# Weighted sum over edges: the weights move from the one-hots to the rows, which are split in two 12-bit parts

## What is computed

```python
msgs = x[edge_src] * edge_val[:, None]
agg = jax.ops.segment_sum(msgs, edge_dst, num_segments=x.shape[0])
return agg @ weight
```

## Time and profile before

| | us |
|---|---|
| median of three executions | 4533.24 |
| lowest, highest | 4529.37, 4536.89 |
| the profiled execution | 4536.84 |
| its span, from the first instruction to the last | 4535.1 |
| the pass, from its first gather to the start of its last addition | 1371.5 to 2025.1 |

### The profile page before, as it was taken

The page is one execution under the profiler, slowest core; times in us unless marked ns, Lnnn a source line. Parts: engine busy times, 40 slices in busy tenths (PEclk is TensorE's granted clock), DMA queues, the critical chain, the costliest instruction groups (busy, mean ns, idle before and its releaser), DMA issues. The chain is left out here.

```text
span 4535.1 us, 63274 instructions
## 1 busy us (share of the span) xinstructions
PE 3412.7 (75%) x19013; PEld 2743.6 (60%) x19013; DVE 2035.7 (45%) x5778; ACT 1546.3 (34%) x4091; POOL 2322.5 (51%) x2297
## 2 busy tenths in 40 slices
PE   3777787624396777774675399997978999998796
PEld 3555555412164555553564399996536888887696
DVE  4666555650144444442322211115346777777523
ACT  3554555410042222221221122221125666665432
POOL 3454555447505666653665544441427788885153
PEclk7888888756697888886788699998869999999698
DMA  6755555200005677660454487774549999997466
GB/s 188 220 163 145 154 159 144 57 11 14 0 24 187 224 234 233 229 203 29 129 167 151 132 246 236 243 241 146 133 125 252 257 262 263 266 264 173 133 214 206
DMA packets 491983, 777.54 MB, mean 171 GB/s; under 512 B 154329, under 2 KB 296994, under 8 KB 491394
## 3 DMA queue, kind: packets, MB, share of 16 engines
q1 hardware_dynamic: 359986, 498.14, 34.8%
q0 software_dynamic: 122608, 266.94, 24.1%
q10 hardware_dynamic: 9056, 8.43, 0.6%
HBM read 599.88 MB, written 173.38 MB: 171 GB/s over the span
## 5 line engine op out<-in xcount | busy, mean ns | idle before, releaser
L874 POOL DMA_INDIRECT sum_rows<-t_row,src_i x416 | 393.9, 947 | 401.5 <-POOLq L2143 157.5
L874 POOL DMA_INDIRECT ag_rows<-t_att,src_i x416 | 401.8, 966 | 378.8 <-DVE ag_msg L985 260.9
L1745 POOL DMA_INDIRECT eg_early<-t_edge,src_i x312 | 487.4, 1562 | 172.0 <-issue 88.5
L286 POOL DMA_INDIRECT t_cells<-times_seen,cell x416 | 404.5, 972 | 265.6 <-issue 126.8
L1065 PE MATMUL ps<-featT,ag_msg 128*128 128x128 f32 x1664 | 364.7, 353 | 126.9 <-issue 116.0
L1793 PE MATMUL ps<-eg_w,eg_rT 128*128 128x256 f32 x1664 | 435.2, 384 | 0.0
L1065 PEld LDWEIGHTS ps<-featT,ag_msg 128*128 128x128 f32 x1664 | 274.7, 235 | 230.2 <-issue 192.5
L1472 PE MATMUL ps<-cv_cells,cv_high 128*128 128x384 f32 (+2 forms) x1200 | 322.7, 349 | 95.4 <-DMA cv_cells<-t_cells 95.4
L971 DVE TENSOR_TENSOR att_sums<-att_sums,ps 128x384 f32 x416 | 228.7, 550 | 323.0 <-remote 148.1
L1113 PE MATMUL ps<-sum_w1g,sum_eaT 64*128 64x256 f32 x1248 | 217.1, 475 | 193.8 <-ACT sum_kept L1157 127.2
L1176 DVE TENSOR_TENSOR featT<-featT,ps 128x256 f32 x416 | 175.3, 421 | 366.0 <-remote 181.1
(11 more groups left out here) (434 smaller groups left out, 6803.8 us busy)
## 6 DMA issues: line engine op xcount, KB each, us to landing
cv_cells<-t_cells SPq DMA_DIRECT2D x225, 384.0 KB
t_pre<-sum_kept SPq DMA_DIRECT2D x156, 512.0 KB
eg_early<-t_pre SPq DMA_DIRECT2D x156, 512.0 KB
t_cells<-zeros SPq DMA_DIRECT2D x21, 1664.0 KB
cv_cells<-t_cells SPq DMA_DIRECT2D x75, 448.0 KB
xn<-in_L_ffn_W SPq DMA_DIRECT2D x57, 512.0 KB
xn<-in_L_ffn_expert_w SPq DMA_DIRECT2D x110, 256.0 KB
ag_trow<-t_dst SPq DMA_DIRECT2D x104, 256.0 KB
```

Source lines behind the costliest of these rows:

```text
L286: nc.gpsimd.indirect_dma_start(out=t_cells, out_offset=bass.IndirectOffsetOnAxis(ap=cell[:, c:c + 1], axis=0), in_=times_seen[:, c:c + 1], ...
L874: nc.gpsimd.indirect_dma_start(out=rows[:, j, :], out_offset=None, in_=table, in_offset=bass.IndirectOffsetOnAxis(ap=src_i[:, n:n + 1], ax ...
L1745: nc.gpsimd.indirect_dma_start(out=early[:, q % ES, n % 2, :], out_offset=None, in_=t_edge, in_offset=bass.IndirectOffsetOnAxis(ap=src_i[: ...
```

## The change

The weights leave the one-hots, which become plain 0 and 1 and are of type float32r. Instead the rows are weighted. ScalarE multiplies a gathered row by its edge's weight and rounds the result to float32r, the upper part `high`. VectorE computes row times weight less `high` in one instruction and rounds it to float32r too, the lower part `low`. Both have rings of HR = 8 buffers. TensorE then makes four float32r matmuls for each chunk where it made two of f32: upper and lower part for each half of the features, added up in PSUM.

The order on the engines changes with it. ScalarE weights chunk n+2 (AHEAD = 2) behind the copy of chunk n's pair. VectorE makes the lower part of chunk n+2 ahead of the addition of chunk n, and the four one-hots of a later lot behind the addition of the lot's last chunk. GpSimd may refill a row buffer after the lower part is made (`low_kept`), not after the product.

```diff
+            HR = 8
-            hot = sb(tag + "_hot", [EC, GR, EC], F32, c)
+            hot = sb(tag + "_hot", [EC, GR, EC], F32R, c)
+            high = sb(tag + "_high", [EC, HR, D], F32R, c)
+            low = sb(tag + "_low", [EC, HR, D], F32R, c)
...
+            AHEAD = 2
...
-                    gathers(pool, table, rows, GR, g.agg_ready)
+                    gathers(pool, table, rows, GR, g.low_kept)
...
-                    for l in range(EARLY):
+                    def keep(l):
                         if l >= KEPT:
                             act.wait_ge(slot_stored[l % KEPT].sem, slot_stored[l % KEPT].at(16 * (l // KEPT)))
                         act.wait_ge(g.pre_ready.sem, g.pre_ready.at(2 * l + 2))
                         nc.scalar.copy(kept[:, l % KEPT], ps[:, AB:AB + 2, :]).then_inc(g.hid_done.sem, 1)
 
+                    def upper_bits(n):
+                        act.wait_ge(gath[n % GR].sem, gath[n % GR].at(16 * (n // GR) + 16))
+                        if n >= HR:
+                            act.wait_ge(g.agg_ready.sem, g.agg_ready.at(n - HR + 1))
+                        nc.scalar.activation(high[:, n % HR, :], rows[:, n % GR, :], ACT.Identity, scale=weight[:, n:n + 1]).then_inc(g.high_kept.sem, 1)
+
+                    for n in range(AHEAD):
+                        upper_bits(n)
+                    for n in range(NCH):
+                        if n % 2 == 0 and not is_late(n // 2):
+                            keep(early_number(n // 2))
+                        if n + AHEAD < NCH:
+                            upper_bits(n + AHEAD)
...
-                            nc.vector.tensor_scalar(hot[:, ER * h + j, :], iota[:], dloc[:, bass.ds(ER * m + j, 1)],
-                                                    weight[:, bass.ds(ER * m + j, 1)], ALU.is_equal, ALU.mult).then_inc(g.one_hot.sem, 1)
...
+                            nc.vector.tensor_scalar(hot[:, n % GR, :], iota[:], dloc[:, n:n + 1], None, ALU.is_equal).then_inc(g.one_hot.sem, 1)
+
+                    def lower_bits(n):
+                        dve.wait_ge(g.high_kept.sem, g.high_kept.at(n + 1))
+                        nc.vector.scalar_tensor_tensor(low[:, n % HR, :], rows[:, n % GR, :], weight[:, n:n + 1], high[:, n % HR, :].bitcast(F32),
+                                                       ALU.mult, ALU.subtract).then_inc(g.low_kept.sem, 1)
...
+                    for m in range(LOTS - 1):
+                        one_hots(m)
+                    for n in range(AHEAD):
+                        lower_bits(n)
+                    for n in range(NCH):
+                        if n % ER == 0:
+                            windows[:] = starts(dve, nc.vector, n // ER)
+                        if n + AHEAD < NCH:
+                            lower_bits(n + AHEAD)
+                        add(n)
+                        if n % ER == ER - 1 and n // ER + LOTS - 1 < NL:
+                            one_hots(n // ER + LOTS - 1)
...
-                        pe.wait_ge(gath[j].sem, gath[j].at(16 * (n // GR) + 16))
+                        pe.wait_ge(g.low_kept.sem, g.low_kept.at(n + 1))
...
-                            lhs = rows[:, j, k * 128:(k + 1) * 128]
-                            mm = nc.tensor.matmul(ps[:, n % BANKS, k * EC:(k + 1) * EC], lhs, hot[:, j, :], start=True, stop=True)
+                            for which, split in enumerate((high, low)):
+                                mm = nc.tensor.matmul(ps[:, n % BANKS, k * EC:(k + 1) * EC], split[:, n % HR, k * 128:(k + 1) * 128], hot[:, j, :],
+                                                      start=(which == 0), stop=(which == 1))
```

More of the change, by code:

```diff
@@ L1162, in _, with one_hots @@
                     dve.wait_ge(g.added.sem, g.added.at(1))
-                    def one_hots(m, i, h, first):
+                    windows = []
+                    def one_hots(m):
                         for j in range(ER):
-                            nc.vector.tensor_scalar(hot[:, ER * h + j, :], iota[:], dloc[:, bass.ds(ER * m + j, 1)],
-                                                    weight[:, bass.ds(ER * m + j, 1)], ALU.is_equal, ALU.mult).then_inc(g.one_hot.sem, 1)
-                    def add(m, i, h, first):
-                        for j, b in enumerate(starts(dve, nc.vector, m)):
```

12 lines of the change are left out of this document (6 added, 6 removed).

## The result

The changed kernel is **slower**: 4623.92 us in the median of three runs (4611.07 to 4623.97) against 4533.24, a ratio of 1.0191 (95% interval 1.0161 to 1.0220). I had forecast 4478 us and a range up to 4556. Its profiled execution is the run of 4623.92 us.

What follows compares the result with a forecast made beforehand. GpSimd's gather issue was taken as the floor, with late TensorE results holding the pass above it: 10.3 + 1.0 = 11.3 us per 8 chunks, 588 + 11 = 599 us against 654, so 4478 us; range 4415 to 4556.

Steps and rivals of the forecast that it cites:

- The price of the products: PE's weighted-sum matmuls: four single-pass products cost 0.27 us per chunk instead of 0.50, with 0.45 as upper end.
- The clock: PE in the edited pass: busy share falls from 70% to about 50%, granted clock 0.77 beside 0.85 before.
- rival 3: PE at 1.2 GHz for most of the pass; ScalarE's copy loop takes 12.5 us per 8 chunks: 4540 us; chance 0.12.
- rival 4: PE: float32r products of 128 columns cost 0.45 us per chunk, PE nearly as busy as now; shares 0.22 with rival 2.
- ScalarE's loop: Copy, attribute products, copy, with weightings queued between: 9.2 us per 8 chunks at the upper clock, about 12.5 at the lower.
- The late results: TensorE's results reaching waiting engines late: 2.5 us of GpSimd's waits per 8 chunks, forecast to fall to 1.0.
- The floor: GpSimd's gather issue: 1.25 us per chunk, 520 us for the pass; taken as 10.3 us per 8 chunks after the change.
- The 134 us: Edited pass: 654 us less GpSimd's 520, explained by GpSimd's waits of 110.9 and 20.8 us.
- number 2: Edited pass: late results stay and hand-overs are added, 24 us more, 4557 us, or 4530; shares chance 0.22 with rival 4.
- the 0.08 us: GpSimd's gathers: lengthened from 0.96 to 1.04 us beside VectorE's instruction with two SBUF inputs.

Runs made afterwards that it cites:

- e17: Changed kernel with gathers replaced by plain DMAs of the table's first 128 rows and splitting six chunks ahead, not two: 4013.4 us, pass 706.
- e18: Changed kernel with plain DMAs for gathers, splitting six chunks ahead, and products of 256 moving columns instead of 128: 3736.9 us, pass 438.
- e1: Changed kernel with each product 256 moving columns wide (both chunks of a pair) instead of 128: 4663.8 us, ratio 1.0172 to the kernel before, pass 746.
- e3: Kernel before with its two F32 products per chunk replaced by four single-pass ones of 128 columns, rows not split: 4632.9 us, ratio 1.0095, pass 715.
- e8: Kernel before with each gather of the pass replaced by a plain DMA of the table's first 128 rows: 4318.0 us, pass 448.
- e9: Kernel before with GpSimd waiting, ahead of every fourth gather, until the gather two before has landed: 4605.2 us, ratio 1.0035, pass 687.
- e13: Kernel before with half of TensorE's work in the pass left out: 4528.6 us beside 4571.7 for the kernel before; gathers over 609 us.
- e10: Kernel before with the gathers' buffers released one by one instead of four at a time: 4585.0 us, pass 661.
- e11: Kernel before with at most three gathers in flight: 4585.3 us, pass 656.
- e14: Kernel before with each store in the pass cut to a sixteenth, full stores made behind the pass: gathers over 642 us; whole time says nothing.
- e15: Kernel before with half of TensorE's work and stores of a sixteenth in the pass: gathers over 616 us; whole time says nothing.
- e4: Changed kernel without the products of the lower part, two single-pass products per chunk instead of four: 4638.1 us, pass 721.
- e16: Changed kernel with each gather of the pass replaced by a plain DMA of the table's first 128 rows: 4028.6 us, pass 732.

## Why the prediction was wrong, step by step

**The price of the products failed first.** I took 0.066 us for a product of 128 columns, scaled down from products of 384 columns, and 0.27 us per chunk. Measured is 0.213 us for each at the lower clock, 0.85 us per chunk. The upper bound that I wrote down, 0.45 us per chunk from the 0.11 us of the 16-column records, is the right one once the clock is counted: 0.107 us at 2.4 GHz would be 0.213 at 1.2. I had the row that told the truth and took the one that I liked. The single-pass product of 128 columns saves no TensorE time at all.

The Trainium skill, page "TensorE: Matmul & The Clock Gate", section "Back-to-back issue gap", gives N / 1.2 GHz from one matmul to the next at the lower clock, without the weight load, which is an estimated 107 ns at 128 columns. The rows of this case, with a weight load for each product, have 213 ns for F32R, and the measurement decides.

**The clock failed next.** It is worth most with plain DMAs (706 against 438 us, e17 and e18), and nothing where announcements are late (e1 has it back and a pass of 746 us). I put 0.77 to 0.85, and against my rival 3 I argued that at the lower clock PE would be 85% busy, "and the rows show it raised then". It is 98% busy, and in e3 and e17 100%, and not raised. No row of mine had PE 85% busy at the lower clock: the busiest stretch in the earlier trace rows has 70%, at 0.85, and it is one of F32 products, with full slots. The busy share in the rows counts a half-empty slot as a full one. Rival 3 and rival 4 were right together, and I had priced each alone: the lower clock on ScalarE's loop (12.5 us per eight chunks, at PE's cheap price), the dear products at the upper clock. Together they give TensorE 13.1 us per eight chunks, which neither had.

**The late results.** "I take it that less than half of the late results remain" was marked as the weakest step. They did go, in full, and it was worth nothing here, since the pass had become slower than they made it. I had said they need a busy PE and gathers without a pause. The second half held (e8, e9), the first didn't: half the PE work leaves them as they are (e13), and the wait of 142.75 us, in the trace that I had, stands beside a PE that is busy 22.81 us of 120.

**The floor.** The forecast summed to 10.3 + 1.0 us per eight chunks, over GpSimd's issue floor of 1.25 us per chunk. (Its own range of late results, 0.4 to 1.6, gives 4447 us at the lower end and not 4455.) On the chips with late announcements nothing with indirect gathers went below 1.47 us per gather, in six attempts (e9 with 1.64, e10, e11, e13, e14, e15) on kernels in which TensorE was not the bound. The 134 us that I called a gap to be closed were not open to this change, nor to any that I tried. Of the rivals, only number 2 had the sentence that mattered ("they come from gathers without a pause, whatever PE does").

**What held.** ScalarE's weighting lasts 0.50 us (priced 0.41 to 0.50) and VectorE's lower part 0.48 (0.48). The loop through ScalarE's copy at the lower clock, "about 12.5 us", shows in e4, where TensorE has half the products: from its copy at 1651.29 us to the one at 1664.44 it is 13.2 us. Two prices were too high. VectorE's one-hots are shorter, four in 0.88 us where they took 1.29 and where I had counted no gain. The gathers did not grow beside the two-input instruction (947 ns), so the 0.08 us that I added from the earlier trace rows was not paid.

**Where the 89 us come from.** TensorE at the lower clock alone makes the pass 706 us (e17) to 715 (e3), 52 to 61 us more than before; by the whole times on its own chip e3 costs 46. The short lead adds 26 (e16 against e17), the gathers 11 (743 against 732). The parts were measured on different chips, so their sum, 89 to 98, fits no better than it should. The parts are not gains to be had one by one, either: with the clock back, late announcements take the place of the slots at the same 746 us (e1). Settled: hand-overs don't hold the clock down. Open: what holds back TensorE's announcements beside indirect gathers, and why one chip is free of it. No version with all its work and faster than the kernel before was found on the chips with late announcements. Wide products with the lead of six are the version to try where gathers run freely; with true gathers that was not run there.

## What to carry to other kernels

Price a single-pass product by the slot it holds, not by its columns, and look for the nearest row in width: here 128 columns cost what 256 do, and filling the slot took the same instructions from 706 to 438 us. Read the busy share and the granted clock together: here a PE at 98% busy and 0.50 did less work than one at 70% and 0.85. Before a forecast counts on a gap above an engine's issue time, look whether any stage of the trace gets below that gap with the same kind of DMA; a wait that can be named is not yet a wait that can be won.

## What the runs showed of the hardware that I had not expected

- F32R products with 128 stationary and 128 moving columns start 0.213 us apart at 1.2 GHz, with 256 moving columns 0.21 us apart at 1.2 GHz too, and 0.12 at 2.4 (e1). With the first the clock stayed at 0.50 over 700 us of an always busy PE (e3, e17); with the second it was 1.00 in e18 from 1000 us to the end of the pass.
- TensorE's announcements came 3 us and more late beside unbroken runs of indirect gathers on all chips but one, at either clock, with half of PE's work, and with a sixteenth of the store traffic. Ahead of the pass, beside unbroken small indirect writes, ScalarE waited 142.75 us for one. Plain DMAs from GpSimd at 339 GB/s did not cause it. Pauses between runs of four gathers ended it, and cost as much.
- One chip ran the kernel before in 3843.9 us, where the others took 4533 to 4590; a gather of the first pass took 1.28 us there instead of 1.86.
